# Graph kernel: one-hot keys by broadcast loads instead of TensorE transposes, 24 looked-up columns in the first layer, first look-ups beside the table's last stores

## The reference

```python
# first layer
h_src = h[src]
e   = concat([h_src @ Ws.T, he @ Ws.T, h[dst] @ Ws.T]) @ Wa.T          # one number per edge
msg = einsum('ei,eio->eo', h_src, W_rel[type_90]) * e                  # 16x16 matrix of the edge's type
x   = layernorm(x + segment_sum(msg, dst))
# second layer
msg = einsum('emh,eh->em', edge_emb[type_8].reshape(-1,16,16), x[src])
m   = segment_sum(msg, dst)
x   = layernorm(x + GRU(m, x))                                         # gates by w_ih, w_hh
```

## Time and profile before

| what | us |
|---|---|
| median of three runs | 6740.62 |
| the profiled execution, its own time | 6727.4 |
| its span, first to last instruction | 6725.4 |
| mean granted TensorE clock | 0.915 of full speed |
| PE busy with matmuls | 5513.0 (82%) |
| DVE busy | 5057.7 (75%) |
| ACT busy | 4653.9 (69%) |
| POOL busy | 3845.6 (57%) |

### The profile page before, as it was taken

The page is one execution under the profiler, slowest core; times in us unless marked ns, Lnnn a source line. Parts: engine busy times, 40 slices in busy tenths (PEclk is TensorE's granted clock), DMA queues, the critical chain, the costliest instruction groups (busy, mean ns, idle before and its releaser), DMA issues.

```text
span 6725.4 us, 111510 instructions
## 1 busy us (share of the span) xinstructions
PE 5513.0 (82%) x37701; PEld 5197.1 (77%) x37701; DVE 5057.7 (75%) x8412; ACT 4653.9 (69%) x5477; POOL 3845.6 (57%) x4053
## 2 busy tenths in 40 slices
PE   4678888888888888889648888888888888888874
PEld 1478888888888888888638888888878888878863
DVE  6588888888888888888727777777776777777763
ACT  5667777777777777777527777777777777777753
POOL 3445555555565555555545555555565555555555
PEclk8789999999999999999859999999999999999985
DMA  9511111111111111111110000000000000000000
GB/s 313 219 27 33 33 30 33 27 33 33 33 33 33 33 33 30 33 27 33 43 47 12 12 14 14 14 14 14 14 14 14 14 14 11 14 14 14 14 17 9
DMA packets 215465, 237.70 MB, mean 35 GB/s; under 512 B 104864, under 2 KB 182123, under 8 KB 214760
## 3 DMA queue, kind: packets, MB, share of 16 engines
q0 software_dynamic: 129504, 37.43, 6.7%
q1 hardware_dynamic: 70170, 115.25, 5.0%
q10 hardware_dynamic: 15726, 84.19, 3.2%
HBM read 71.21 MB, written 164.99 MB: 35 GB/s over the span
## 4 chain that ended last, share of the span: by engine, by line
PE 42%; ACT 22%; another core or an unknown queue 19%; issue 7%; DVE 6%; DMA 1%; ACTq 1%; DVEq 0%; POOL 0%; SPq 0%; POOLq 0%
PE ps_table L725 35%; ACT hot L895 13%; ACT hot L899 6%; PE ps_table L735 4%; PE ps_misc L707 3%; ACT hot L896 3%; DVE t_buf L1238 1%; DVE t_buf L1248 1%; DVE work L1244 1%; DVE scanned L1202 1%; DMA relation_table<-t_buf 1%; PE ps_table L843 0%; DMA relation_table<-scanned 0%; ACTq L863 0%
## 5 line engine op out<-in xcount | busy, mean ns | idle before, releaser
L725 PE MATMUL ps_table<-node_halves,hot 128*128 128x320 f32 x27040 | 4467.0, 323 | 727.3 <-ACT hot L899 309.0
L725 PEld LDWEIGHTS ps_table<-node_halves,hot 128*128 128x128 f32 x27040 | 4216.5, 198 | 872.1 <-issue 638.2
L895 ACT ACTIVATE hot<-ps_misc,less_key 128x512 fp32r<-128x512 f16 (+1 forms) x3640 | 2069.0, 660 | 1664.6 <-remote 1150.3
L557 POOL DMA_INDIRECT rows<-relation_table,idx x1872 | 1782.9, 952 | 1286.0 <-PE ps_table L725 721.2
L557 POOL DMA_INDIRECT rows<-type_table,idx x1872 | 1771.4, 946 | 1263.0 <-PE ps_table L725 697.1
L899 ACT ACTIVATE hot<-hot,ones 128x3072 fp32r<-128x3072 f32 (+1 forms) x728 | 1949.9, 2678 | 23.7
L1238 DVE TENSOR_TENSOR t_buf<-ps_table,work 128x640 f32<-128x640 f32 (+1 forms) x1456 | 1107.6, 767 | 1066.7 <-PE ps_table L725 790.7
L1244 DVE TENSOR_REDUCE work<-t_buf 128x64 f32<-128x1280 f32 (+1 forms) x728 | 1012.6, 1391 | 25.0
L1248 DVE TENSOR_TENSOR t_buf<-ps_table,work 128x1024 f32<-128x1024 f32 (+1 forms) x728 | 836.0, 1148 | 159.9 <-remote 74.0
L1252 DVE TENSOR_REDUCE rows<-t_buf 128x64 f32<-128x1024 f32 (+1 forms) x728 | 833.3, 1145 | 25.1
L707 PE MATMUL ps_misc<-ident_f,match_cols 128*128 128x128 f16 x5408 | 436.9, 222 | 93.7 <-ACT hot L896 42.3
(11 more groups left out here) (203 smaller groups left out, 1602.4 us busy)
## 6 DMA issues: line engine op xcount, KB each, us to landing
scanned<-scanned ACTq DMA_DIRECT2D x52, 992.0 KB
relation_table<-scanned SPq DMA_DIRECT2D x50, 765.0 KB
relation_table<-t_buf SPq DMA_DIRECT2D x48, 765.0 KB
rows<-relation_table,idx POOLq DMA_INDIRECT x1872
rows<-type_table,idx POOLq DMA_INDIRECT x1872
scanned<-scanned ACTq DMA_DIRECT2D x52, 496.0 KB
he<-in_edge_attr SPq DMA_DIRECT2D x48, 496.0 KB
type_table<-t_buf SPq DMA_DIRECT2D x14, 448.0 KB
```

Source lines behind the costliest of these rows:

```text
L557: pool.indirect_dma_start(out=rows[:, k, :], out_offset=None, in_=table, in_offset=bass.IndirectOffsetOnAxis(ap=index[:, k:k + 1], axis=0) ...
L725: last = pe.matmul(ps_banks[:, c, 0:BLOCK_W], hot[:, b, g, edges], node_halves[:, half, g, :, :].rearrange("p f j -> p (f j)"), start=(g = ...
L895: act.activation(hot[:, b, g, edges], match_bank[:, 0, edges], ACT.Abs, bias=less_key[:, g:g + 1])
```

## The change

**Keys and types by broadcast loads.** Source indices and types of the looked-up columns are handed over a second time by the host, laid out so that one set's edges are one contiguous row in HBM. DVE makes all chunks' keys at once in the table stage (`edge_keys`), ACT stores them as `key_rows` (f16), and for every set SP loads the row of keys (f16) and the row of types (int32) to all 128 partitions, into a ring of three slots at the end of `whole`. ACT's `Abs` read the slots. PE's transposes, the signals `match_ps` and the PSUM bank are gone. `keys` keeps the part that `hot_tile` needs.

**First layer 24 columns.** `GROUPS_OF[0]` is (4, 4, 4, 4, 4, 4); POOL gathers 38 columns there. The second layer keeps 26 and 36. The scans are spread over six sets.

**Start.** ACT itself issues the first three sets' loads behind its last table copy, and DVE makes chunk 0's keys before it waits for the table's stores. PE's two flag matmuls (L695) and what DVE does with them move behind chunk 0.

**Pacing.** The gathers of chunk 0 of either layer no longer wait for look-ups.

**By the way.** With the ring in `whole`, `end_rows` works in parts of at most 14 columns of 62, and the second `halve_nodes` uses `scanned` as scratch.

```diff
-GROUPS_OF = ((4, 4, 4, 4, 4, 3, 3), (4, 4, 4, 4, 4, 3, 3))
+GROUPS_OF = ((4, 4, 4, 4, 4, 4), (4, 4, 4, 4, 4, 3, 3))
+SLOTS = 3
...
+    def slot_free(self, m, parity, q):
+
+        at, cycle = self.at(parity, q), 2 * self.quads
+        before = next(k for k in range(1, cycle + 1) if (at - k) % cycle % SLOTS == at % SLOTS)
+        return m * self.quads + (q + 1 - before)
...
+        def spread_quad(eng, lay, m, parity, q):
+
+            wait_past(eng, match_sb[lay.n], lay.slot_free(m, parity, q))
+            at, count = lay.row_at(q)
+            s, landed = lay.slot(parity, q), ring_in[q]
+            for rows, place in ((key_rows, ring_keys[s]), ((rows_90, rows_8)[lay.n], ring_types[s])):
+                eng.dma_start(place[:, 0:count], rows[bass.ds(m, 1), at:at + count].to_broadcast([P, count])
+                              ).then_inc(landed, 16)
...
             with sp.Fori(1, FULL // 2) as i:
-                pair(i)
+                for h in range(2):
+                    edges(i, h)
+                    spread_chunk(layers[0], i * 2 + h, h)
...
+            for q in range(SLOTS):
+                spread_quad(sp, layers[1], 0, 0, q)
...
                 def wait(k):
+                    if isinstance(m, int) and m == 0:
+                        return
                     if k == 0 or lay.columns_before(k) > lay.columns_before(k - 1):
...
-            def spread_quad(lay, m, parity, q):
-
-                pe.wait_ge(keys_set[lay.n], m + 1)
-                wait_past(pe, match_sb[lay.n], m * lay.quads + q)
-                for k in range(2):
-                    for c in range(lay.groups[q]):
-                        at = lay.first[q] + c
-                        last = pe.transpose(match_bank[:, k, c * P:(c + 1) * P],
-                                            match_cols[:, parity, k, at:at + 1].to_broadcast([P, P]), ident_f16[:, :])
-                last.then_inc(match_ps[lay.n], 1)
...
                 for q in range(lay.quads):
-                    if q < lay.quads - 1:
-                        spread_quad(lay, m, parity, q + 1)
-                    elif not last:
-                        spread_quad(lay, m + 1, 1 - parity, 0)
                     for duo in range(QUAD // DUO):
...
-            with act.Fori(1, TILES // 4) as i:
+            with act.Fori(1, KEYS_BY) as i:
                 four(i)
-
+            act.wait_ge(key_rows_set, 1)
+            act.dma_start(key_rows.rearrange("m e -> (m e)").rearrange("(p c) -> p c", p=P), key_flat
+                          ).then_inc(key_rows_out, 16)
+            with act.Fori(KEYS_BY, TILES // 4) as i:
+                four(i)
+
+            act.wait_ge(key_rows_out, 16)
+            act.wait_ge(whole_free, 1)
+            for q in range(SLOTS):
+                spread_quad(act, layers[0], 0, 0, q)
 
             def one_hot(lay, m, parity, q):
 
                 quad = m * lay.quads + q
-                act.wait_ge(match_ps[lay.n], quad + 1)
+                s = lay.slot(parity, q)
+                act.wait_ge(ring_in[q], lay.loads_done(m, q))
                 wait_past(act, products_ps[lay.n], lay.quads_done(m, q - 2))
...
-                    act.activation(hot[:, b, g, edges], match_bank[:, 0, edges], ACT.Abs, bias=less_key[:, g:g + 1])
-                act.activation(hot[:, b, BLOCKS, edges], match_bank[:, 1, edges], ACT.Abs,
+                    act.activation(hot[:, b, g, edges], ring_keys[s][:, edges], ACT.Abs, bias=less_key[:, g:g + 1])
+                act.activation(hot[:, b, BLOCKS, edges], ring_types[s][:, edges], ACT.Abs,
...
+            def edge_keys():
+                dve.wait_ge(src_rows_in, 16)
+                step(dve.tensor_scalar(key_work, src_flat, P.bit_length() - 1, None, ALU.logical_shift_right))
+                step(dve.tensor_scalar(key_work, key_work, float(FIFTH), None, ALU.mult))
+                step(dve.tensor_scalar(key_work, key_work, FIFTH_BITS, None, ALU.logical_shift_right))
+                dve.scalar_tensor_tensor(out=key_flat, in0=key_work, scalar=-float(BLOCKS * P), in1=src_flat,
+                                         op0=ALU.mult, op1=ALU.add).then_inc(key_rows_set, 1)
...
-            SCAN_WITH = (range(0), range(6), range(6, 12), range(12, 17), range(17, 22), range(22, 27), range(27, 2 * D))
+            SCAN_WITH = (range(0), range(7), range(7, 14), range(14, 20), range(20, 26), range(26, 2 * D))
```

More of the change, by code:

```diff
@@ L18, with __init__ @@
 QUAD, DUO = 4, 2
-GROUPS_OF = ((4, 4, 4, 4, 4, 3, 3), (4, 4, 4, 4, 4, 3, 3))
+GROUPS_OF = ((4, 4, 4, 4, 4, 4), (4, 4, 4, 4, 4, 3, 3))
 LEAD = 2
+SHARE = max(sum(groups) for groups in GROUPS_OF)
+SLOTS = 3
 class Layer:
-    def __init__(self, n, edge_types, kinds, strips, mats, rows):
+    def __init__(self, n, edge_types, kinds, strips, mats, rows, chunks):
         self.n, self.edge_types, self.kinds = n, edge_types, kinds
@@ L98, in build @@
     assert BLOCK_W <= 512 and DUO < BANKS and DUO * D * D <= 512
-    SHARE = max(sum(groups) for groups in GROUPS_OF)
     STATE_RUNS = TILES * D // CHUNK
@@ L363, in runs_view, with in_parts @@
             return rows.bitcast(I32)[:, 0:count * CHUNK].rearrange("p (t c) -> p t c", c=CHUNK)
+        def in_parts(rows, first_tile):
+            return [(rows[:, k:min(k + MARKS, rows.shape[1]), :], first_tile + k)
+                    for k in range(0, rows.shape[1], MARKS)]
         run_parts = [
@@ L513, in _ @@
                 pair(i)
+            spread_chunk(layers[1], 0, 0, SLOTS)
+            spread_chunk(layers[1], 1, 1)
+            with sp.Fori(1, PAIRS) as i:
+                for h in range(2):
+                    spread_chunk(layers[1], i * 2 + h, h)
             sum_edges(1, scan1, D)
@@ L749, in chunk_by_products @@
                     products(lay, m, parity, q)
-            spread_quad(layers[0], 0, 0, 0)
+            pe.wait_ge(t0_sb, TILES)
             chunk_by_products(layers[0], 0, 0, False)
+            pe.wait_ge(flags_set, 1)
+            for k in range(2):
+                last = pe.matmul(ps_misc[0:2 * D, k * P:(k + 1) * P], flag_cols[:, k, :], ident[:, :],
+                                 start=True, stop=True)
+            last.then_inc(flags_ps, 1)
             def pair(i, last=False):
@@ L1341, in runs_done @@
                     dve.wait_ge(runs_step, k)
-                for n, (rows, first_tile) in enumerate(run_parts):
+                mark_parts = [part for rows, first_tile in run_parts for part in in_parts(rows, first_tile)]
+                for n, (rows, first_tile) in enumerate(mark_parts):
                     count = rows.shape[1]
```

142 lines of the change are left out of this document (89 added, 53 removed).

## The result

| | us | of before |
|---|---|---|
| before, 20 runs | 6742.24 median (6718.52 to 6758.82) | |
| changed, 20 runs | 6755.07 median (6737.63 to 6778.18) | 1.0022 (95%: 1.0012 to 1.0033) |
| forecast | 6503 (6310 to 6830) | 0.965 |

What follows compares the result with a forecast made beforehand. Prediction: PE's signals, held back while POOL issues gathers without a pause, lengthen every chunk. Terms -120 (second layer), -138 (first), +2 (start), +16 (chunk 0), +2 (end_rows) = -238 on 6727.4: 6489, plus 13 for the median: 6503 us, range 6310 to 6830.

Steps and rivals of the forecast that it cites:

- within 1 us of 11 a chunk: Sign of the forecast in both layers: ACT's idling for "remote", PE's late signals, stays at about 11 us a chunk.
- a sign that I had named: Sign against the forecast: first-layer chunk over 59 us with PE waiting "remote" behind runs of more than six gathers.
- held signals: In both layers, PE's signals reach ACT late while POOL issues without a pause; some 11 us a chunk idle "remote".
- The transposes and ACT's reading: Both layers: dropping PE's transposes saves 2.8 us a chunk, ACT's SBUF reading costs 0.5; -2.3 us a chunk.
- 24 columns: First layer: PE saves 3.45 us, POOL's two more gathers cost 2.5, holding 0.6; -0.35 us a chunk, bounds -3.45 and +3.3.
- Chunk 0 unpaced: First chunk of each layer: gathers without a pause delay PE's signals; +8 us a layer, 16 in all, bounds 0 and +24.
- The loads: Key and type loads on SP: about 0.2 more DMA share, landed ahead of use, costed at nothing.
- The start: Before the first look-up: earlier first block saves 6.5 us against DVE's passes and queue traffic; +2 us, bounds -6.5 and +7.
- PE's relief is eaten: Rival, no change: a lighter PE shortens nothing, -0.3 us a chunk in each layer, one-offs +20; 6730 us, chance 0.13.
- gathers set the pace: Rival, slower: a chunk is POOL's issuing plus pauses, whatever PE does; first layer grows 170 us; 6930 us, chance 0.17.
- POOL's waiting per gather: First layer: staying at 0.44 us while PE is ready decides for "gathers set the pace"; forecast: waits from 15.7 to about 11 us.
- the rule of the Trainium skill: DMA never contends with a compute engine, so denser gathers would not slow PE; 6320 us, within a rival of chance 0.14.

Runs made afterwards that it cites:

- A: Kind of run on one chip, used only in the first of five rounds, where the kernel before takes 6742.31 us.
- e2: Changed kernel with 26 instead of 24 looked-up columns and 36 gathers in the first layer; on A 6709.15 us, 0.9952 of the kernel before.
- B: Kind of run on four other chips, where the kernel before takes 5710.24, 5711.24, 5712.64 and 5711.88 us.
- e11: Kernel before with 24 looked-up columns in the first layer, a second time; on B 5542.72 us, 0.9705 of the kernel before.
- e9: The changed kernel itself, run again beside the kernel before; on B 5500.99 us, 0.9632 of the kernel before.
- e16: Changed kernel with the pacing of chunk 0 restored in both layers; on B 5505.21 us, 0.9637 of the kernel before.
- e5: Changed kernel with 26 looked-up columns in the first layer and chunk 0 paced; on B 5693.04 us, 0.9969 of the kernel before.
- e10: Same kernel as e5, a second time; on B 5691.07 us, 0.9964 of the kernel before.
- e14: Same kernel as e5, once more; on B 5692.65 us, 0.9967 of the kernel before.
- e1: Changed kernel with the pacing of chunk 0 restored in both layers; on A 6710.27 us, 0.9956 of the kernel before.

## Why the prediction was wrong

**The bound.** On A "remote" stayed, and the forecast step "within 1 us of 11 a chunk" was missed on both sides (13.4 and 9.5). Half of a sign that I had named came: the first layer's chunk is over 59 us, but PE's waits there are mostly "issue", not "remote". What I did not draw from the held signals is the consequence: POOL's chunk is issuing plus pauses, and PE's relief hardly shortens the pauses. POOL's waiting fell by 1.7 us a chunk in each layer; the forecast had it fall by 4.7 in the first. That a pause is as long as held work needs to get through, whatever PE's own need is, fits these numbers, but no run on A tests it outside chunk 0.

**The transposes and ACT's reading (-2.3 us a chunk; -120 and -120 us).** This step failed: I took 0.43 us of PE per set for 0.43 us of the chunk. On A the transposes' going gave 0.4 us a chunk in the first layer (58.6 to 58.2, before against e2) and 1.1 in the second (57.8 to 56.7). The second layer from its chunk 1 to the end says the same: 63.8 us saved, 1.25 for each of 51 chunks. Kind B shows the part that no held signal explains. In the first layer, where DVE is the full engine, the transposes' going gives 0.1 us: 48.7 us a chunk with them (e11) and 48.5 without (e9), both with 24 columns, from POOL's rows between 400 and 2700 us. In the second layer PE is the fullest engine before (2042.59 of 2100 us between 3100 and 5200, e11), and after the change ACT is (1997.16, against PE's 1968.14, e9). So only the distance to ACT can be saved. ACT in the second layer on B, the kernel before with 24 first-layer columns (2967 to 5337 us):

```profile
L895 ACT ACTIVATE hot<-ps_misc,less_key 128x512 fp32r<-128x512 f16 x1275 | 763.9, 691 | 97.8 <-PE ps_misc L707 97.6
L899 ACT ACTIVATE hot<-hot,ones 128x3072 fp32r<-128x3072 f32 x255 | 730.2, 2863 | 8.3
L895 ACT ACTIVATE hot<-ps_misc,less_key 128x384 fp32r<-128x384 f16 x510 | 251.5, 585 | 98.0 <-PE ps_misc L707 98.0
L899 ACT ACTIVATE hot<-hot,ones 128x2304 fp32r<-128x2304 f32 x102 | 226.6, 2222 | 3.3
L896 ACT ACTIVATE hot<-ps_misc,less_type 128x512 fp32r<-128x512 f16 x255 | 182.0, 714 | 0.0
L896 ACT ACTIVATE hot<-ps_misc,less_type 128x384 fp32r<-128x384 f16 x102 | 61.9, 607 | 0.0
```

and the changed kernel (2955 to 5295 us):

```profile
L961 ACT ACTIVATE hot<-whole,less_key 128x512 fp32r<-128x512 f16 x1273 | 807.0, 710 | 23.4 <-PE ps_table L790 23.4
L965 ACT ACTIVATE hot<-hot,ones 128x3072 fp32r<-128x3072 f32 x255 | 730.5, 2865 | 8.3
L961 ACT ACTIVATE hot<-whole,less_key 128x384 fp32r<-128x384 f16 x510 | 269.3, 604 | 80.3 <-PE ps_table L790 80.3
L965 ACT ACTIVATE hot<-hot,ones 128x2304 fp32r<-128x2304 f32 x102 | 226.8, 2223 | 3.3
L962 ACT ACTIVATE hot<-whole,less_type 128x512 fp32r<-128x512 int32 x255 | 180.8, 709 | 0.0
L962 ACT ACTIVATE hot<-whole,less_type 128x384 fp32r<-128x384 int32 x102 | 61.4, 602 | 0.0
```

Over 51 chunks ACT's work in these groups is 43.45 us a chunk before and 44.62 after, of a chunk of 46.5 and 45.9, and its wait for PE falls from 3.8 to 2.0. So the transposes give 1.8, reading SBUF takes 1.2 back, and 0.6 remains. I had counted ACT's price at a half; where ACT is the full engine it is paid whole. Its size was right, 1.1 us a chunk forecast and 1.2 measured: five `Abs` in a row take 3.17 us where they took 3.00 (the earlier trace rows and the start's row below). By its own duration an `Abs` is only 19 ns longer (691 to 710), not 29, and the type's instruction 5 ns shorter; the rest is the distance from one `Abs` to the next.

**24 columns (-0.35 us a chunk).** e2 against the changed kernel makes it +46 / 52 = +0.9 us on A over the whole span, +1.4 clear of the first chunks. I had given the saving of 3.45 us of PE its whole size and taken it against POOL's 2.5; on A the time shows nothing of PE's half set. On B the columns are worth -3.2 us a chunk in the kernel before and (5505 - 5692) / 52 = -3.6 in the changed one with chunk 0 paced (e16 against e5, e10, e14). That is a little beyond my bound of -3.45; clear of the first chunks it is -3.3 (51.8 in e5, 48.5 in e9), beside DVE's own work of 50.1 and 46.9 us a chunk (DVE's busy time from 400 to 2700 us by POOL's chunks). It is DVE's work that is saved, and not PE's. The forecast itself had DVE at 50.4 us in the first layer and PE at 47.6, and its sum has no term for DVE; of ACT's need it gives no number.

**Chunk 0 unpaced (16 us).** 45 us (e1). The price was taken from the run of gathers between the layers, where PE had little to do. Beside look-ups PE itself stands between its matmuls, and the bound of 24 a layer held, the choice of 8 did not.

**The loads (nothing).** 27 us on A, nothing that counts on B (5 us). On A ACT waits for a load only before the first block of each layer; the second time is between the layers, long before that block is needed. In e9 four more such waits stand in the first layer, 19.3 us together, beside DVE as the full engine. **The start (+2)**: -1.6. The first block begins at 265.97 instead of 267.77, while the last stores end 5.9 us later, the upper price of DVE's four passes; no run separates these from the traffic of the keys:

```profile
265.97 3.17 ACT L961 ACTIVATE hot<-whole,less_key 128x512 fp32r<-128x512 f16 x5 [7.75 <-DMA whole<-rows_edge_type]
266.39 1.71 DVE L1272 MEMSET scanned<- 128x1984 f32 x1 [11.92 <-DMA relation_table<-scanned]
```

**The rivals.** "PE's relief is eaten" (6730) came nearest, with the first layer on the side of "gathers set the pace". The point that I named for the latter, POOL's waiting per gather, fell in between: 14.0 / 38 = 0.37 us, where 0.44 had been the mark for no relief and 11 / 38 = 0.29 was forecast. By the rule of the Trainium skill (SBUF — State Buffer, section Who interferes with whom) gathers would not slow PE. On B this is what the runs show (12 us for 32 to 34 gathers a chunk). On A, PE beside a run of gathers issues a matmul every 2.1 to 2.8 us; the measurement decides.

**That the ratio came out on B** is no support for the sum: its terms were read from A's held trace, and there they failed. The agreement is luck: 24 columns gave -3.2 us a chunk instead of -0.35, and the transposes 0.1 and 0.6 instead of 2.3 in each layer. With 26 columns, where only the loads for the transposes and the start are left of the change, B gains 0.3 to 0.4% (e5, e10, e14).

## What to carry to other kernels

When a chain has a share that no engine owns, first ask what it pays for: here PE's saved time vanished while the chunk kept the length of GpSimd's issuing and pauses. List every engine's own need, price an edit on the fullest one, and stop the saving where the next engine becomes the fullest: on B that was DVE in the first layer and ACT in the second, and the sum asked neither how much it lets through. And a trade between gathers and matmuls is worth a look on more than one chip: 24 columns instead of 26 were 3% faster on one kind of chip and 0.7% slower on the other.
